# One low half by subtraction on VectorE, and a new order of work on every engine

## The chip, the cores and the metric

The kernel runs on one core of a Trainium2 chip. The metric is the device time of one execution in microseconds, the median of three runs. A profile is one more execution, taken with the hardware profiler; its span runs from the first to the last instruction. Engines: TensorE (PE), VectorE (DVE), ScalarE (ACT), GpSimd (POOL), SyncE (SP, which here only issues transfers).

## The reference

Input `x` is 4 batches of 512 rows by 512, `ctx` 4 batches of 512 by 256. All is float32.

```python
# cross attention
query = ctx @ Wq.T + bq; key = ctx @ Wk.T + bk           # per batch 512 x 128
attention = softmax(query @ key.T)                        # 512 x 512
x = x + layernorm(x) @ attention.T
# feed-forward on 2048 rows, each matrix first rounded block-wise to FP8
def mx_dequant(t):                                        # blocks of 32 along a row
    s = max(max_abs(block) / 448, 1e-30); return fp8_e4m3(t / s) * s
n = layernorm(x)
h = silu(mx(n) @ mx(gate_w).T) * (mx(n) @ mx(up_w).T)     # 2048 x 2048
x = x + mx(h) @ mx(down_w).T
```

## The kernel before

**Units, rows, hidden rows.** The three weight matrices come as twelve `units` of 128 x 2048 (0 to 7 gate and up, in four column groups of 512, two units each; 8 to 11 down). A unit is loaded into one of three buffers `W`, reduced to block maxima (`unit_reduce`, `unit_largest`), scaled (`unit_scale`), rounded to FP8's grid (`unit_round`, after ScalarE's `unit_magnitude`), scaled back (`unit_dequant`). A dequantized value does not fit float16, so it is split: ScalarE writes the high half, minus the value as float16 (`unit_hi`); then value plus high half is left over, and that is the low half. The sum is made by a transfer that GpSimd issues with `accum_op=add` (`unit_rest`), and ScalarE writes it as float16 (`unit_lo`). Both halves are turned by transposing transfers from SyncE (`turn_unit_hi`, `turn_unit_lo`) into `gu_hi`, `gu_lo` or `dn`. The four batches of normalized rows go the same way (`center`, `rows_scale`, `rows_round`, `rows_dequant`, `rows_hi`, `rows_rest`, `rows_lo`, `turn_rows_hi`, `turn_rows_lo`, into `xT`, which has places for two batches), and so do the sixteen hidden row tiles (`hidden_...`, into `hT`, places for two tiles). For hidden tiles 7 to 15 (`hidden_by_vector`) VectorE makes the low half from value and high half by one subtraction, and there is no accumulating transfer. Buffers are shared between the stages, so many waits are on a place that must come free.

**TensorE.** `project`, `energies`, `turn_probs` (transposes the softmax's rows and weighs them) and `attend` are float32 matmuls: attention. `product(r, c)` is row tile r (batch r // 4) times column group c, gate and up, 24 float16 matmuls; it waits for the batch's turned high half, and after 8 matmuls for the low half. `down(r)` is 48 matmuls with hidden tile r. The stages are interleaved: `product(3,0)` is the first product, `product(6,0)` the first with rows of batch 1. Eleven matmuls on zeros stand at the start. All results pass through the eight banks of PSUM; which bank each use takes, and so what it waits for, is written out in `bank_uses`.

**Order.** Each engine has one queue, written out call by call; SyncE's holds all loads, stores and transposes, with waits among them (`sp.wait_ge(*unit_rest_in(4))` ahead of `turn_rows_hi(1)`). GpSimd's holds the maxima over partitions (`unit_max`), the accumulating transfers, `second_norm(b)` (a power, the reciprocal root of batch b's variance, for b from 1), and the accumulating stores of the result (`add_out`). ScalarE makes statistics of x (`row_means`, `row_variances`), the exponentials, `take_probs` (bank to `AT`), `silu_of`. VectorE makes `row_max`, `row_sum`, `add_attended` (x plus attention), `hidden_of` (silu times up). Every wait is a semaphore against a constant count.

The low half's two ways are already there for rows:

```python
def rows_lo_done(b):
    if b in rows_by_vector:
        return nlo_made, ...
    return nlo_ready, ...
```

Of the kernel before, what the change touches and what calls it, by code (L numbers as in the profile page):

```python
# [13 lines left out]
P = 128  # L14
# [18 lines left out]
def xattn_ffn(nc, xrows, xcols, ctxT, consts, units, out):  # L33
# [35 lines left out]
        ("p0.0 p2.0 e2.0 a0.3 a1.0 a2.2 g1.0 a3.2 g2.1 g4.1 u6.2 g0.2 u0.3 u3.3 u7.1 g8.0 u9.1 g11.0 u12.0 u14.2"  # L69
         " u13.1 g8.2 u10.2 u15.0 d9").split(),  # L70
        ("p0.1 e1.0 e2.1 t1.0 a1.1 t3.0 g0.0 u2.0 g4.0 u2.2 g0.1 u6.3 u1.3 g7.1 d0 g9.1 u10.0 d4 g10.3 u15.1 d11").split(),
        ("e0.0 e1.1 t0.3 a0.2 e3.0 t2.2 a2.0 g3.0 u1.0 g6.0 u4.1 u3.2 u0.2 u1.1 g4.3 u7.2 u8.0 g9.3 g11.1 g12.1"
         " g14.2 u13.0 g12.3 u10.1 d6 g15.3 d14").split(),
        ("e0.1 e1.2 a0.0 t1.3 a1.3 t3.3 a3.3 u2.1 g5.0 g5.1 g5.3 g1.2 u4.2 g7.3 g8.1 g9.2 u11.0 u12.1 g14.3 g13.1"
         " u12.3 g10.2 g15.0 u15.2 d13").split(),
        ("e0.2 e1.3 a0.1 t2.0 t2.3 a2.1 u3.0 g2.0 g6.1 u5.0 g5.2 u5.3 g1.3 u4.3 u7.3 g9.0 u9.3 u11.2 u14.1 g13.0"
         " u13.3 g10.1 u11.3 g15.2 d12").split(),
        ("e0.3 t0.0 t0.2 e2.2 t1.1 t2.1 e3.3 t3.1 u0.0 u6.0 g2.2 u5.1 g6.3 u1.2 g7.0 g2.3 u8.1 g10.0 g11.2 u14.0"
         " u12.2 g13.3 u8.3 g11.3 d8 d15").split(),
        ("p1.0 p2.1 t0.1 p3.1 t1.2 a1.2 t3.2 a3.0 g3.1 u6.1 g6.2 u5.2 g0.3 g3.3 u7.0 u2.3 u9.0 d2 d3 g12.0 g14.1"  # L80
         " g12.2 u13.2 g8.3 d5 g15.1 u15.3").split(),
        ("p1.1 p3.0 e2.3 e3.1 e3.2 a2.3 a3.1 u3.1 u4.0 g3.2 u0.1 g1.1 g4.2 g7.2 d1 u9.2 u11.1 g14.0 u14.3 g13.2"
         " u8.2 u10.3 d7 d10").split(),
# [3 lines left out]
    rows_by_vector = ()  # L87
    logged = (0,)
    stats_by_vector = ()
    slice_size = 256  # L90
    hidden_by_vector = (7, 8, 9, 10, 11, 12, 13, 14, 15)

    with ExitStack() as stack:
# [237 lines left out]
        def _(sp):  # L331
# [13 lines left out]

            def load_consts():
                sp.dma_start(late[:, 1024:1538 + P], consts).then_inc(consts_in, 16)
# [114 lines left out]
            turn_unit_hi(0)  # L462
            load_unit(3)
            turn_unit_lo(0)
            load_rows(3)
            store_rows(0)
            sp.wait_ge(*unit_rest_in(1))
            turn_unit_hi(1)
            load_columns(2)
            load_unit(4)  # L470
            turn_unit_lo(1)
            turn_unit_hi(2)
            load_columns(3)
            sp.wait_ge(*rows_rest_in(0))
# [5 lines left out]
            store_rows(2)  # L480
# [3 lines left out]
            load_unit(6)  # L484
            store_rows(3)
# [26 lines left out]
            turn_unit_hi(10)  # L512
            reload_rows(2)
            turn_unit_lo(10)
            turn_unit_hi(11)
            sp.wait_ge(*hidden_rest_in(0))
            turn_unit_lo(11)
# [10 lines left out]
            turn_hidden_hi(2)  # L528
            sp.wait_ge(*hidden_rest_in(3))
            turn_hidden_lo(2)  # L530
            turn_hidden_hi(3)
            turn_hidden_lo(3)
            load_last()
            sp.wait_ge(*rows_rest_in(3))
            turn_hidden_hi(4)
            turn_hidden_lo(4)
            turn_hidden_hi(5)
            turn_rows_hi(3)
            turn_rows_lo(3)
# [11 lines left out]
            turn_hidden_lo(10)  # L551
            turn_hidden_hi(11)
            turn_hidden_lo(11)
# [16 lines left out]
        def _(pool):  # L570
# [34 lines left out]
            unit_max(0)  # L605
            unit_rest(0)
            unit_max(1)
            unit_max(2)
            pool.wait_ge(wT_in[1], 16)
            unit_rest(1)  # L610
            pool.wait_ge(wT_in[0], 48)
            unit_rest(2)
            rows_rest(0)
# [9 lines left out]
            unit_max(6)  # L623
            pool.wait_ge(wT_in[1], 80)
            unit_rest(5)
            unit_max(7)
            pool.wait_ge(wT_in[1], 96)
            unit_rest(6)
            unit_max(8)
            pool.wait_ge(wT_in[1], 112)  # L630
            unit_rest(7)
            unit_max(9)
            pool.wait_ge(wT_in[1], 128)
            unit_rest(8)
# [42 lines left out]
        def _(pe):  # L677
# [104 lines left out]
            energies(0, 0)  # L782
            energies(0, 1)
            energies(0, 2)
            energies(0, 3)
            project(1, 0)
            project(1, 1)
            project(2, 0)
            energies(1, 0)
            project(2, 1)  # L790
            energies(1, 1)
            project(3, 0)
            energies(1, 2)
            energies(1, 3)
            turn_probs(0, 0)
            energies(2, 0)
            turn_probs(0, 1)
            energies(2, 1)
            turn_probs(0, 2)
            turn_probs(0, 3)  # L800
# [3 lines left out]
            attend(0, 1)  # L804
            attend(0, 2)
            energies(2, 3)
            attend(0, 3)
            turn_probs(1, 0)
            turn_probs(1, 1)
# [3 lines left out]
            energies(3, 0)  # L813
            energies(3, 1)
            attend(1, 0)
            attend(1, 1)
            turn_probs(2, 1)
# [4 lines left out]
            energies(3, 2)  # L822
            energies(3, 3)
# [15 lines left out]
            product(2, 0)  # L839
# [38 lines left out]
            product(11, 0)  # L878
            product(11, 1)
            product(11, 2)  # L880
            down(3)
# [20 lines left out]
            down(6)  # L902
            product(15, 0)
            product(15, 1)
            down(7)
            down(8)
            product(15, 2)
# [10 lines left out]
        def _(act):  # L918
# [223 lines left out]
            act.wait_ge(consts_in, 16)  # L1142
            take_projection(0, 0)
            take_projection(0, 1)
            row_means(0, 0)
            row_means(0, 1)
            unit_magnitude(0)
            unit_rescale(0)
            take_projection(1, 0)
            exponential(0, 0)  # L1150
            take_projection(1, 1)
            exponential(0, 1)
            row_variances(0, 0)
# [24 lines left out]
            exponential(2, 0)
            unit_rescale(1)
            exponential(2, 1)  # L1180
            row_variances(0, 1)
            exponential(2, 2)
            row_means(2, 0)
            take_projection(3, 1)
            unit_hi(1)
            weigh(1, 2)
            unit_magnitude(2)
            exponential(2, 3)
            take_probs(1, 0)
            weigh(1, 3)  # L1190
            unit_rescale(2)
            weigh(2, 0)
            take_probs(1, 1)
            take_probs(1, 2)
            take_probs(1, 3)
            weigh(2, 1)
            row_means(3, 0)
            unit_lo(1)
            attended_variances(0, 0)
            row_variances(1, 0)  # L1200
            row_means(2, 1)
            row_variances(2, 0)
            rows_magnitude(0)
            unit_hi(2)
            weigh(2, 2)
            attended_variances(0, 1)
            exponential(3, 0)
            weigh(2, 3)
            take_probs(2, 0)
            exponential(3, 1)  # L1210
            take_probs(2, 1)
            take_probs(2, 2)
            take_probs(2, 3)
            row_variances(1, 1)
            rows_hi(0)
            exponential(3, 2)
            row_means(3, 1)
            row_variances(3, 0)
            exponential(3, 3)
            row_variances(2, 1)  # L1220
            weigh(3, 0)
            weigh(3, 1)
            weigh(3, 2)
            weigh(3, 3)
            unit_magnitude(3)
            rows_lo(0)
# [742 lines left out]
```

## Time and profile before

| | |
|---|---|
| median of three runs | 611.02 us (610.16 to 611.29) |
| the profiled execution | 610.0 us |
| its span | 608.0 us |
| TensorE busy / mean granted clock | 600.6 us (99%) / 0.999 |
| VectorE busy | 484.0 us (80%) |
| ScalarE busy | 309.2 us (51%) |
| GpSimd busy | 44.8 us (7%) |
| matmuls in the trace | 2683 |
| transfers: SyncE's share of 16 engines, GpSimd's | 45.2%, 19.9% |

Busy time of an engine is from its first to last cycle of each instruction; matmuls overlap, and a busy TensorE is one with no hole. VectorE's 80% is an average: it is over 97% in most slices before 260 us and near nothing from 410 to 450.

### The profile page before, as it was taken

The numbers are of one execution on the slowest core, as the hardware profiler recorded it, in microseconds if no ns is written. First come the engines' busy times: TensorE is split into PE (matmuls) and PEld (weight loads), VectorE is DVE, ScalarE is ACT, GpSimd is POOL, SyncE is SP. The second block draws the span as 40 slices with busy tenths as digits, with TensorE's granted clock in tenths as the row PEclk, the third lists the DMA queues.
The fourth block names the chain that finished last, engine by engine and source line by source line (L and its number), as shares of the span: only waits on it lengthen the run. The fifth ranks groups of instructions, "written<-read, shape, count | busy, mean of one in ns | idle before, by whom it ended". The sixth has DMA issues, their size and how long they took to land.

```text
span 608.0 us, 7215 instructions
## 1 busy us (share of the span) xinstructions
PE 600.6 (99%) x2683; PEld 282.3 (46%) x2683; DVE 484.0 (80%) x455; ACT 309.2 (51%) x463; POOL 44.8 (7%) x60
## 2 busy tenths in 40 slices
PE   8999999999999999999999999999999999999998
PEld 3456554444444444444444444444444444444446
DVE  4999998899999999988999985131148899989740
ACT  3999989553555555853475532431121515254520
POOL 0000002100000001010110201000000000001100
PEclk9999999999999999999999999999999999999999
DMA  8989869989988978867445655750010334557691
GB/s 314 396 206 275 234 177 256 280 193 249 208 207 209 219 159 210 174 140 171 124 112 97 148 112 113 165 86 0 1 19 0 53 69 83 90 105 101 110 171 35
DMA packets 148162, 92.28 MB, mean 152 GB/s; under 512 B 134304, under 2 KB 134688, under 8 KB 143264
## 3 DMA queue, kind: packets, MB, share of 16 engines
q1 hardware_dynamic: 142656, 63.78, 45.2%
q0 software_dynamic: 5472, 28.05, 19.9%
q8 instruction: 21, 0.34, 0.2%
q14 instruction: 13, 0.11, 0.1%
HBM read 25.76 MB, written 8.39 MB: 56 GB/s over the span
## 4 chain that ended last, share of the span: by engine, by line
PE 85%; DMA 5%; issue 3%; ACT 3%; DVE 1%; SPq 1%; POOL 0%; DVEq 0%; ACTq 0%
PE bank L727 49%; PE bank L739 17%; PE bank L742 9%; PE bank L711 5%; DMA h<-in_ctxT 2%; PE bank L702 1%; PE bank L695 1%; DMA xT<-hT 1%; PE bank L687 1%; PE bank L757 1%; DMA W<-hT 1%; DMA h<-hT 1%; ACT hT L944 1%; PE bank L762 1%; ACT h L987 0%
## 5 line engine op out<-in xcount | busy, mean ns | idle before, releaser
L727 PE MATMUL bank<-gu_hi,xT 128*128 128x512 f16 x1024 | 243.6, 380 | 1.7 <-DMA xT<-hT 1.7
L727 PEld LDWEIGHTS bank<-gu_hi,xT 128*128 128x128 f16 x1024 | 99.9, 98 | 123.4 <-DMA xT<-hT 3.2
L727 PE MATMUL bank<-gu_lo,xT 128*128 128x512 f16 x512 | 131.5, 379 | 0.0
L739 PE MATMUL bank<-dn,hT 128*128 128x512 f16 x480 | 106.1, 379 | 0.0
L1633 DVE SCALAR_TENSOR_TENSOR h<-bank,unscale,silu 128x512 f32<-128x512 f32 x64 | 47.4, 747 | 56.1 <-PE bank L727 36.1
L1088 ACT ACTIVATE silu<-bank,unscale 128x512 f32<-128x512 f32 x64 | 42.8, 679 | 83.4 <-PE bank L727 40.3
L727 PEld LDWEIGHTS bank<-gu_lo,xT 128*128 128x128 f16 x512 | 50.1, 98 | 60.4
L739 PEld LDWEIGHTS bank<-dn,hT 128*128 128x128 f16 x480 | 47.0, 98 | 56.6
L1114 ACT ACTIVATE W<-h 128x2048 f16<-128x2048 f32 x16 | 30.5, 1909 | 68.3 <-DVE W L1665 25.4
L711 PE MATMUL bank<-dn,h 128*128 128x512 f32 x128 | 55.9, 593 | 0.0
L742 PE MATMUL bank<-dn,hT 128*128 128x512 f16 x240 | 54.3, 379 | 0.0
L1458 DVE SCALAR_TENSOR_TENSOR h<-mag,h 128x2048 f32<-128x2048 bf16 x18 | 41.2, 2288 | 9.4 <-ACT mag L926 9.4
L926 ACT ACTIVATE mag<-h 128x2048 bf16<-128x2048 f32 x18 | 34.2, 1903 | 19.5 <-DVE h L1647 14.1
L1459 DVE SCALAR_TENSOR_TENSOR h<-mag,h 128x2048 f32<-128x2048 bf16 x18 | 41.2, 2292 | 0.6
L926 ACT ACTIVATE mag<-W 128x2048 bf16<-128x2048 f32 x14 | 26.7, 1908 | 23.0 <-DVE W L1590 11.9
L711 PEld LDWEIGHTS bank<-dn,h 128*128 128x128 f32 x128 | 24.3, 190 | 29.8 <-issue 29.4
L1665 DVE SCALAR_TENSOR_TENSOR W<-h,W 128x2048 f16<-128x2048 f32 x9 | 20.6, 2289 | 20.9 <-DMA hT<-W 17.4
L1647 DVE TENSOR_TENSOR h<-h,rscale 128x2048 f32<-128x2048 f32 x16 | 36.7, 2292 | 0.5
L1642 DVE TENSOR_REDUCE hscale<-h 128x64 f32<-128x2048 f32 x16 | 36.5, 2281 | 0.3
L1659 DVE TENSOR_TENSOR h<-h,hscale 128x2048 f32<-128x2048 f32 x16 | 36.6, 2288 | 0.2
L742 PEld LDWEIGHTS bank<-dn,hT 128*128 128x128 f16 x240 | 23.5, 98 | 28.3
L1458 DVE SCALAR_TENSOR_TENSOR W<-mag,W 128x2048 f32<-128x2048 bf16 x14 | 32.0, 2286 | 1.0 <-ACT mag L926 1.0
(119 smaller groups left out, 560.1 us busy)
## 6 DMA issues: line engine op xcount, KB each, us to landing
W<-hT POOLq DMA_DIRECT2D x12, 1024.0 KB, 5.9
W<-in_units SPq DMA_DIRECT2D x11, 1024.0 KB, 5.7
h<-W POOLq DMA_DIRECT2D x7, 1024.0 KB, 6.1
h<-in_xcols SPq DMA_DIRECT2D x4, 1024.0 KB, 12.6
out_y<-y POOLq DMA_DIRECT2D x12, 256.0 KB, 6.2
h<-in_xrows SPq DMA_DIRECT2D x2, 1024.0 KB, 11.8
out_y<-h SPq DMA_DIRECT2D x2, 1024.0 KB, 5.5
h<-hT POOLq DMA_DIRECT2D x2, 1024.0 KB, 5.9
```

The source lines that it names most:

```text
L711: last = pe.matmul(bank[:, :], xTf[b % 2][:, j, lt * P:(lt + 1) * P], AT[:, j, :], start=(j == 0), stop=(j == HT - 1))
L727: last = pe.matmul(bank[:, :], xT[:, b % 2, part, k, :], w[:, c, g, j * 512:(j + 1) * 512], start=(j == 0 and not low), stop=(j == HT - 1 ...
L739: pe.matmul(bank[:, :], hT[:, r % 2, 0, k, :], dn[:, w, k, :], start=(k == 0 and w == 0), stop=False)
L742: last = pe.matmul(bank[:, :], hT[:, r % 2, 1, k, :], dn[:, 0, k, :], start=False, stop=(k == IT - 1))
L926: nc.scalar.activation(mag[:, :], v, ACT.Abs, scale=MAGIC).then_inc(mag_ready, 1)
L1088: nc.scalar.activation(silu[:, n % 2, :], bank_of(f"g{r}.{c}")[:, :], ACT.Silu, scale=unscale[:, 2 * c:2 * c + 1]).then_inc(silu_ready, 1)
L1458: then(dve.scalar_tensor_tensor(v, mag[:, :], floor, v, ALU.max, ALU.add))
L1459: dve.scalar_tensor_tensor(v, mag[:, :], floor, v, ALU.max, ALU.subtract).then_inc(mag_used, 1)
L1633: dve.scalar_tensor_tensor(hrow(r)[:, c * 512:(c + 1) * 512], bank_of(f"u{r}.{c}")[:, :], unscale[:, 2 * c + 1:2 * c + 2], silu[:, n % 2, ...
L1642: then(dve.tensor_reduce(s, blocks(row), AX.X, ALU.max, apply_absolute_value=True))
L1647: dve.tensor_tensor(blocks(row), blocks(row), each_block(rscale[:, :]), ALU.mult).then_inc(hv_ready, 1)
L1659: dve.tensor_tensor(blocks(row), blocks(row), each_block(hscale[:, r % 2, :]), ALU.mult).then_inc(hd_ready, 1)
```

## The change

Batch 0's rows join `rows_by_vector`: VectorE runs its `rows_lo(0)` (shown below), GpSimd's `rows_rest(0)` and ScalarE's `rows_lo(0)` are gone, and SyncE no longer waits for `rows_rest_in(0)`. A switch `apart`, left off, could load part of the constants first. And the calls on all five queues, with the banks, are in a new order; no call but those named is added or removed. At the start, the constants are loaded ahead of the first context tile, and the other context tiles ahead of the rows:

```diff
-    rows_by_vector = ()
+    rows_by_vector = (0,)
@@ SyncE
 load_slice(0)
+load_consts()
 load_ctx(0)
-load_consts()
 load_half(0)
 load_rest(0)
-load_rows(0)
 load_ctx(1)
 load_unit(1)
+load_ctx(2)
 load_ctx(3)
-load_ctx(2)
+load_rows(0)
+load_columns(0)
 load_rows(1)
+load_rows(2)
 load_unit(2)
-load_columns(0)
-load_rows(2)
 load_columns(1)
...
+sp.wait_ge(*unit_rest_in(2))
 turn_unit_hi(2)
-load_columns(3)
-sp.wait_ge(*rows_rest_in(0))
 turn_rows_hi(0)
 turn_rows_lo(0)
 store_rows(1)
 turn_unit_lo(2)
 load_unit(5)
-store_rows(2)
 sp.wait_ge(*unit_rest_in(3))
 turn_unit_hi(3)
 turn_unit_lo(3)
 load_unit(6)
+store_rows(2)
 store_rows(3)
 sp.wait_ge(*unit_rest_in(4))
 turn_rows_hi(1)
@@ GpSimd
-pool.wait_ge(wT_in[0], 48)
+pool.wait_ge(wT_in[1], 32)
 unit_rest(2)
-rows_rest(0)
@@ TensorE
+turn_probs(3, 0)
+turn_probs(3, 1)
 attend(2, 0)
 ...
 attend(2, 3)
-turn_probs(3, 0)
-turn_probs(3, 1)
 turn_probs(3, 2)
-turn_probs(3, 3)
 product(3, 0)
 product(1, 0)
+turn_probs(3, 3)
 product(0, 0)
+product(2, 0)
 attend(3, 0)
 ...
 attend(3, 3)
-product(2, 0)
@@ VectorE
 rows_round(0)
+unit_power(3)
 rows_dequant(0)
 add_attended(1, 0)
 ...
 add_attended(1, 3)
+rows_lo(0)
+attended_means(1)
 unit_reduce(4)
...
 rows_dequant(1)
+unit_power(4)
+add_attended(2, 1)
 unit_round(4)
-hidden_of(3, 0)
+add_attended(2, 2)
+add_attended(2, 3)
 unit_dequant(4)
...
 hidden_of(15, 3)
+hidden_scale(15)
 hidden_round(14)
+hidden_lo(13)
 hidden_dequant(14)
-hidden_scale(15)
-hidden_lo(13)
 hidden_round(15)
```

The subtraction that VectorE now runs for batch 0, in code that was there and unused:

```python
def rows_lo(b):
    dve.wait_ge(nhi_ready, b + 1)
    if b % 2 == 1:
        dve.wait_ge(nT_in[1], 16 * b)
    parts = xparts_of(b)
    dve.scalar_tensor_tensor(parts[:, 1, :], xw_of(b), -1.0, parts[:, 0, :],
                             ALU.mult, ALU.subtract).then_inc(nlo_made, 1)
```

Between `silu_of(3,0)` and batch 1's variance ScalarE's new order is: `silu_of(3,0)`, `center_by_scalar(1,1)`, `take_probs(3,1)`, `take_probs(3,2)`, `weigh(3,3)`, `unit_hi(3)`, `attended_variances(1,0)`, `attended_variances(1,1)`. Before, it was `silu_of(3,0)`, `take_probs(3,0)`, `attended_variances(1,0)`, `unit_hi(3)`, `take_probs(3,1)`, `attended_variances(1,1)`, with both halves of `center_by_scalar(1)` ahead.

## Rows read from the trace of the kernel before

**Rows 1.** page, part 1: TensorE's busy time
```profile
PE 600.6 (99%) x2683; PEld 282.3 (46%) x2683; DVE 484.0 (80%) x455; ACT 309.2 (51%) x463; POOL 44.8 (7%) x60
```

**Rows 2.** TensorE in order of time: start, length, line, count, [idle before, releaser]
```profile
18.58 1.96 PE L687 MATMUL bank<-h,gu_lo 128*128 128x512 f32 x4 [0.79 <-DMA h<-in_ctxT]
...
35.24 10.46 PE L711 MATMUL bank<-dn,h 128*128 128x512 f32 x24
...
74.20 13.90 PE L711 MATMUL bank<-dn,h 128*128 128x512 f32 x32
87.94 3.73 PE L702 MATMUL bank<-h,gu_lo 128*128 128x128 f32 x32
92.60 1.04 PE L727 MATMUL bank<-gu_hi,xT 128*128 128x512 f16 x4 [0.93 <-DMA xT<-hT]
...
94.99 1.90 PE L727 MATMUL bank<-gu_hi,xT 128*128 128x512 f16 x8 [0.49 <-DMA xT<-hT]
...
138.57 1.04 PE L727 MATMUL bank<-gu_hi,xT 128*128 128x512 f16 x4 [0.32 <-DMA xT<-hT]
```

**Rows 3.** the chain that ended last: start, length, what
```profile
77.34 5.10 issue
82.44 5.75 DMA h<-hT
...
104.51 6.03 issue
...
124.79 5.83 DMA W<-hT
130.63 7.89 DMA xT<-hT
138.57 134.85 PE bank L727 x624
...
584.23 6.91 PE bank L739 x32
```

**Rows 4.** ScalarE in order of time, around batch 1's variance
```profile
75.44 1.89 ACT L1074 ACTIVATE hT<-h 128x2048 f16<-128x2048 f32 x1
...
92.34 2.54 ACT L1059 ACTIVATE h<-h,nmean 128x512 f32<-128x512 f32 x4
...
96.70 1.28 ACT L1088 ACT_TABLE_LOAD   x1
...
104.29 0.21 ACT L1044 ACTIVATE var<-ysum 128x4 f32<-128x4 f32 x1
```

**Rows 5.** GpSimd in order of time: start, length, line, [idle before]
```profile
71.57 0.85 POOL L585 DMA_DIRECT2D W<-hT  x1 [23.09 <-DMA gu_hi<-hT]
82.44 0.88 POOL L589 DMA_DIRECT2D h<-hT  x1 [10.01 <-issue]
...
110.53 1.89 POOL L580 TENSOR_TENSOR rstd<-var,mhalf 128x4 f32<-128x4 f32 x1 [6.75 <-issue]
```

**Rows 6.** the twelve accumulating transfers of `unit_rest` (L585), issue to landing
```profile
DMA to landing us min/median/max: 5.8/5.9/10.6
```

**Rows 7.** page, part 5: groups, busy us, mean ns of one
```profile
L926 ACT ACTIVATE mag<-W 128x2048 bf16<-128x2048 f32 x14 | 26.7, 1908 | 23.0 <-DVE W L1590 11.9
...
L1665 DVE SCALAR_TENSOR_TENSOR W<-h,W 128x2048 f16<-128x2048 f32 x9 | 20.6, 2289 | 20.9 <-DMA hT<-W 17.4
```

**Rows 8.** VectorE in order of time, its two longest holes before 123
```profile
106.88 2.29 DVE L1458 SCALAR_TENSOR_TENSOR h<-mag,h 128x2048 f32<-128x2048 bf16 x1 [2.31 <-ACT mag L926]
...
112.52 0.23 DVE L1549 TENSOR_TENSOR xscale<-xscale,rstd 128x64 f32<-128x64 f32 x1 [1.02 <-POOL rstd L580]
```

**Rows 9.** SyncE's queue at the end: hidden row 14, high and low
```profile
577.65 3.19 SPq L439 DMA_TRANSPOSE hT<-W  x1
580.93 1.93 SPq L444 DMA_TRANSPOSE hT<-W  x1
```

**Rows 10.** the four transposes of rows' high halves (L420), issue to landing
```profile
DMA to landing us min/median/max: 4.3/4.6/7.9
```

More of the change, by code:

```diff
@@ L804, in _ @@
             attend(0, 1)
+            energies(2, 3)
+            turn_probs(1, 0)
+            energies(3, 0)
             attend(0, 2)
-            energies(2, 3)
+            turn_probs(1, 1)
+            energies(3, 1)
             attend(0, 3)
-            turn_probs(1, 0)
-            turn_probs(1, 1)
             turn_probs(1, 2)
@@ L812, in _ @@
             turn_probs(2, 0)
-            energies(3, 0)
-            energies(3, 1)
+            turn_probs(2, 1)
+            energies(3, 2)
             attend(1, 0)
+            energies(3, 3)
             attend(1, 1)
-            turn_probs(2, 1)
             attend(1, 2)
@@ L901, in _ @@
             product(11, 3)
-            down(6)
             product(15, 0)
             product(15, 1)
+            down(6)
+            product(15, 2)
             down(7)
             down(8)
-            product(15, 2)
             down(9)
@@ L1197, in _ @@
-            row_means(3, 0)
+            exponential(3, 0)
+            row_means(2, 1)
+            unit_rescale(2)
+            exponential(3, 1)
+            weigh(2, 2)
+            attended_variances(0, 0)
+            weigh(2, 3)
+            row_variances(1, 1)
             unit_lo(1)
-            attended_variances(0, 0)
-            row_variances(1, 0)
-            row_means(2, 1)
+            exponential(3, 2)
             row_variances(2, 0)
+            exponential(3, 3)
+            unit_hi(2)
@@ L1231, in _ @@
-            unit_lo(2)
-            silu_of(3, 0)
-            take_probs(3, 0)
+            unit_magnitude(3)
+            row_variances(3, 1)
+            take_probs(3, 0)
+            unit_lo(2)
+            center_by_scalar(1, 0)
+            silu_of(3, 0)
+            center_by_scalar(1, 1)
+            take_probs(3, 1)
+            take_probs(3, 2)
+            weigh(3, 3)
+            unit_hi(3)
             attended_variances(1, 0)
-            unit_hi(3)
-            take_probs(3, 1)
             attended_variances(1, 1)
-            take_probs(3, 2)
+            silu_of(1, 0)
@@ L1366, in _ @@
-            hidden_rescale(7)
-            hidden_hi(6)
-            silu_of(11, 2)
+            hidden_lo(4)
+            take_down(2)
+            hidden_magnitude(6)
+            hidden_rescale(5)
+            hidden_rescale(6)
+            hidden_hi(5)
+            rows_lo(3)
+            silu_of(11, 0)
+            hidden_lo(5)
+            hidden_unscale(3)
+            silu_of(11, 1)
+            hidden_unscale(4)
+            hidden_magnitude(7)
+            hidden_rescale(7)
+            hidden_unscale(5)
@@ L1439, in _ @@
             take_down(14)
+            hidden_unscale(15)
         @block.vector
@@ L1684, in _ @@
             unit_scale(0)
-            unit_power(0)
+            unit_reduce(1)
             row_max(0, 0)
@@ L1758, in _ @@
             add_attended(3, 2)
+            hidden_of(1, 0)
             add_attended(3, 3)
-            hidden_of(1, 0)
+            unit_reduce(6)
+            hidden_of(0, 0)
             unit_scale(5)
-            hidden_of(0, 0)
-            unit_reduce(6)
+            unit_largest(6)
+            unit_scale(6)
+            unit_power(5)
             unit_round(5)
-            unit_largest(6)
-            unit_power(5)
-            unit_scale(6)
             unit_dequant(5)
@@ L1771, in _ @@
             unit_round(6)
+            hidden_of(2, 1)
             unit_reduce(7)
-            hidden_of(2, 1)
+            hidden_of(6, 0)
+            hidden_of(6, 1)
             unit_largest(7)
@@ L1777, in _ @@
             unit_dequant(6)
-            hidden_of(6, 0)
+            unit_power(7)
             unit_round(7)
-            hidden_of(6, 1)
             unit_reduce(8)
```

520 lines of the change are left out of this document (249 added, 271 removed).

## The prediction

> **What bounds the kernel now.** I read the page's busy times first, then who waited for whom, then TensorE's order of time, and last the chain followed back from the end. TensorE is busy 600.6 of 608.0 us and its mean granted clock is 0.999 (the 2.4 GHz level) [rows 1]. No edit adds or removes a matmul, so the time after is TensorE's work plus its holes. The holes that an order can fill are few: 0.79 us for the third context tile (`ctx(2)`), 0.93 and 0.49 at the first `product(3,0)` (both for batch 0's transposed rows), and 0.32 at 138.57, where `product(6,0)` waits for batch 1's transposed rows [rows 2]. After 138.57 there is none. So the end is fixed by when `product(6,0)` starts, provided that nothing later is late; I call that time T. It is 138.57 before. The profiled execution took 610.0 us with a span of 608.0, and the three timed runs have a median of 611.02: I add a change of T to the median. 0.2% of that is 1.2 us, about what a measurement can tell from no change.
>
> The chain says what T hangs on [rows 3]: batch 1's variance leaves ScalarE at 104.5; GpSimd's power starts 6.03 us later and takes 1.90; then (from 112.5) VectorE dequantizes the rows, rounds and dequantizes unit 4; ScalarE writes unit 4's high half; the accumulating transfer takes 5.83; and only behind that transfer does SyncE issue `turn_rows_hi(1)`, whose transpose lands after 7.89. Once T has come, TensorE runs on at 134.85 us for 26 products, 5.18 each. This is a chain of VectorE and transfers under a TensorE that looks full.
>
> **The change, part by part.** (1) Batch 0's low half. Removed: `rows_rest(0)`, issued at 82.44 although ScalarE's high half was written at 77.3 [rows 4]. It stood 5.10 us behind GpSimd's previous transfer, `unit_rest(2)`, issued at 71.57 and landing 10.6 us later, at 82.2; then it took 5.75 itself [rows 3, 5, 6]. Removed too: ScalarE's `rows_lo(0)`, 1.90 us. Added: a subtraction on VectorE, 2.29 us, the price of the nine of that form [rows 7]. So the low half is ready one pass (2.2 us, back to back) behind the high half instead of 10.85 + 1.9. The Trainium skill (DMA: Bandwidth & Descriptors, Issuing engines are not separate DMA queues) says that transfers from all engines run on the same 16 DMA engines and interleave. By that rule `rows_rest(0)` should have started at 77.3 and shared; the trace disagrees for these two, since the second starts only when the first has landed. By the rule the removal saves the transfer alone (5.75), by the row 10.85; neither alters T, which is batch 1's.
>
> (2) VectorE has 5.88 us of holes between 10 and 122.4 (0.98, 0.76, 0.57, 0.24, 2.31, 1.02; the largest in [rows 8]), and is otherwise full there, so the added 2.2 us must fit in these holes or delay everything behind it.
>
> (3) The orders on five queues. Contexts 1 to 3 are loaded ahead of the rows, which removes the 0.79: `project(2,0)` now comes after energies(1,1), at about 19.3, and its tile ends 3.98 MB into SyncE's queue instead of 5.56 (sums of the tiles' sizes). I walked the new order by hand, with durations from before: projection 1.72 and energies 0.86 (four and two matmuls of 0.43, the spacing of attend's 32 in 13.74), attend 3.44, turn_probs 0.92, product 5.18; 2.2 per big VectorE pass and 1.8 per ScalarE pass (the mean less 0.1, since passes overlap at their ends), 0.6 from the end of matmuls to their reader [rows 2, 3, 7]. `attend(0,0)` comes out at about 34.3 (35.24 before), and `product(3,0)` at S = 92.60 - 0.93 - 0.79 - 0.92 (turn_probs(3,3) is moved behind two products) = 90.0. Batch 0's rows: VectorE now does unit 3's scale, row maxima and rows_scale(0) in another order, `rows_dequant(0)` ends at 79.9 (73.1 before), the high half at 82.6, the subtraction at 84.9. SyncE first waits for `unit_rest(2)` (80 to 82), turns unit 2, and then turns the rows: hi lands at about 88.5, lo at 91. They are wanted at 90.0 and 91.7. So the 0.93 and 0.49 go too, with about a microsecond to spare. TensorE's lead when it comes to `product(6,0)` is 0.79 + 0.93 + 0.49 + 0.32 = 2.5, so it could start it at 136.0.
>
> (4) But batch 1's chain. Before, ScalarE's queue took 104.50 - 96.70 = 7.8 from the table load of silu(3,0) to the variance [rows 4]. The new order has the same work in it and half a centering more (2.54 / 2, 1.22 net) and one weigh (0.29): 9.3. It begins when the gate is there, S + 2.6 + 0.6 = 93.2, so the variance leaves at 102.5, 2.0 before its old time. GpSimd: +6.03 + 1.90 = 110.4. VectorE is free by then (rows_round(1) ends at 109.8). It then does rows_dequant(1) 2.47, unit_power(4) 0.27, add_attended(2,1) 0.75, unit_round(4) 4.53, two add_attended 1.34, unit_dequant(4) 2.20 = 11.56: 122.0. Before, the same stretch held only hidden_of(3,0) between them, so 1.7 of the 2.0 gained is given back by the three additions and the power. unit_hi(4) 1.92 and 0.37 to the issue: 124.3; +5.83 = 130.1; +7.89 = T = 138.0 [rows 3, 5]. I add 0.6 for the couplings of the walk that were within 0.4 us (attend(1,0), turn_probs(3,0) and attend(2,0) each wait on a ScalarE instruction that ends 0.2 to 0.4 before it is wanted), and 0.2 for `store_rows(2)`, which now leaves at 120 and not at 104.6, 7.3 us long alone, mostly over before unit 4's transfer moves data. T = 138.8.
>
> New waits on the way: attend(3,2) needs the bank that add_attended(2,2) frees at 119.4, and TensorE comes there at 118.5; 0.9 us, but it comes out of the lead of 2.5 and costs nothing. load_unit(3) now waits for unit_lo(0), which is at 43.8 instead of 38.8, while unit_reduce(3) moves from 73.1 to 50.2: 43.9 + 5.7 = 49.6, so 0 if it lands so, 1 to 2 us of VectorE if not.
>
> (5) Everything behind 140 moves little. Walked in the same way: VectorE ends unit 5's dequantization at 144.1 in both; rows 2 are turned about 4 us later, but their transpose (280.5 and 282.4 before) still lands about 289 and 292, wanted at 294.0 and 295.7; batch 3's comes earlier. The end is the closest: hidden row 14 is turned high at 577.65 and wanted at 584.07, low at 580.93 and wanted at 590.97, with 4.5 to land [rows 3, 9]. In the new order hidden_scale(15) precedes round(14), but rows 8 to 13 run ahead, and I get the high half out at 575.9 and lo at 583.1, so 3 us to spare each. Cost zero; if VectorE were 4 us later, it would be 1 us.
>
> **The rivals.** *The lead is given back* (my forecast): T = 138.8, so +0.2: 611.2. It holds for T between 137.4 and 139.7. *The lead is kept*: the transpose of batch 1 lands in 4.6 us, the median of its four, and not 7.9 [rows 3, 10]. Then T = 138.8 - 3.3 = 135.5, TensorE is the later at 136.0 and the time is 611.0 - 2.5 = 608.5; half of it (T = 137.4) decides for faster. Against it: store_rows(3) still leaves at 127, just ahead of it. *The chain is later*: an accumulating transfer takes 10.6 as `unit_rest(2)` did and not 5.8 [rows 6]. On unit 4 that puts T at 138.8 + 4.8 = 143.6 and the time at 616.0; on unit 2 it is what I counted. A part of it, 0.9 us or more (unit 3's load late, batch 0's transposes late, so that S and all behind it move), decides for slower: T = 139.7 to 141.5, 612.2 to 613.9. *The change does nothing* for the stalls at product(3,0): unit_rest(2) lands after 84 and SyncE holds the rows behind it; then S = 91.4, the chain moves with it, T = 139.5 to 140.2, 612.0 to 612.6.
>
> The Trainium skill (GPSIMD Engine Reference, Specifications) says that GpSimd's SBUF interfaces contend with VectorE instructions that have two SBUF inputs. The added subtraction is one more, so at most its own 2.3 us on a transfer then being set up; here GpSimd has none pending at 82.7, and no term hangs on it.
>
> **How the numbers follow.** Lead given back 0.40, kept 0.28, later 0.22, nothing gained at product(3,0) 0.10. The walk is some 300 steps, each good to 0.1 us, so both sides are open. Faster by over 1.2 us: 0.28, from the second. Within: 0.40 from the first, and 0.03 of the last. Slower: the rest, 0.29. The likeliest time is 611.2, its own range 609.8 to 612.2. The range is 608.7 to 614.8: down to the full lead (608.5) less a hair, up to most of a slow transfer (616.0) cut, which leaves out 2 in 10.
>
> **What would show it.** Right: the wait for ctxT (0.79) gone; attend(0,0) at 34 to 34.6; product(3,0) near 90 with little wait; power of batch 1 at 108 to 109; unit 4's accumulating transfer at 124 to 125; one wait for xT at `product(6,0)`, now 1.5 to 3 us, the new first stall of size; no wait after it. Wrong: a wait of ScalarE or VectorE before attend(2,0), a wait of TensorE after 140, above all at dn/hT near 553 to 595, or unit 4's transfer before 123.

## The result, and the profile after

Before 609.88 us (21 runs, 608.36 to 611.29), after 611.74 us (21 runs, 610.37 to 613.63); ratio 1.0034, 95% interval 1.0025 to 1.0043. The kernel became 0.34% slower, some 2 us, where no measurable change was forecast (611.2 on a median of 611.02). One of e3's twelve runs below (631.0 us, clock 0.949) and one of e8's (910.7 us, clock 0.656) fell into a slower state of the chip and stay out of every median, ratio and count. The profiled execution of after took 613.63 us with a span of 611.8 (before 610.0 and 608.0).

The head first: the page's busy times, then TensorE in order of time up to `product(6,0)`.

```profile
PE 602.4 (98%) x2683; PEld 282.5 (46%) x2683; DVE 486.8 (80%) x456; ACT 306.7 (50%) x462; POOL 53.3 (9%) x59
```

```profile
34.50 7.03 PE L721 MATMUL bank<-dn,h 128*128 128x512 f32 x16
...
89.81 1.03 PE L737 MATMUL bank<-gu_hi,xT 128*128 128x512 f16 x4
...
118.96 7.13 PE L721 MATMUL bank<-dn,h 128*128 128x512 f32 x16 [0.50 <-DVE dn L1513]
...
137.20 1.04 PE L737 MATMUL bank<-gu_hi,xT 128*128 128x512 f16 x4 [0.75 <-DMA xT<-hT]
```

TensorE is busy 1.8 us longer than in [rows 1] with the same 2683 matmuls; the clock, below, accounts for 1.7 of it. The first `attend` stands at 34.50 (before 35.24), `product(3,0)` (L737) at 89.81 with no wait (before 92.60 with 0.93), and T, the start of `product(6,0)`, is 137.20 (before 138.57, [rows 2]). So 1.4 us were won by T. The chain into T, start, length, what:

```profile
121.81 1.92 ACT hT L954
123.73 0.29 issue
124.02 6.14 DMA W<-hT
130.17 0.02 issue
130.18 6.97 DMA xT<-hT
```

The same two transfers as in [rows 3] lead to T, 6.14 and 6.97 long.

The 0.50 at 118.96 is the wait for a bank that the prediction put at 0.9; it comes out of the lead.

Now who TensorE waited for in the whole span: instruction, releaser, us in total, times, longest.

```profile
PE bank L749 <- DMA hT<-W: 2.6, 1, 2.6
PE bank L786 <- DVE dn L1689: 1.2, 1, 1.2
PE bank L705 <- ACT gu_lo L966: 0.8, 1, 0.8
PE bank L737 <- DMA xT<-hT: 0.7, 1, 0.7
```

The largest is new: before had no wait behind T. It is in `down` (L749 the high half's 32 matmuls, L752 the low half's 16), near the end, TensorE in order of time:

```profile
572.37 7.07 PE L749 MATMUL bank<-dn,hT 128*128 128x512 f16 x32
579.92 3.63 PE L752 MATMUL bank<-dn,hT 128*128 128x512 f16 x16 [0.48 <-DMA hT<-W]
586.13 8.75 PE L749 MATMUL bank<-dn,hT 128*128 128x512 f16 x32 [2.59 <-DMA hT<-W]
594.72 3.62 PE L752 MATMUL bank<-dn,hT 128*128 128x512 f16 x16
```

Read it so: `down(13)` starts 1.3 us ahead of before's, waits 0.48 for its low half; `down(14)` waits 2.59 for its high half; and its 32 matmuls then take 8.75 where the 32 above took 7.07. The last group of matmuls begins at 606.91 (before 603.16): -1.37 + 0.48 + 2.59 + 1.68 = +3.4 of the +3.75. In what follows `hi(r)` and `lo(r)` are the two halves of hidden tile r: on ScalarE and VectorE the step that makes one, on SyncE the transpose that turns it; `scale(r)`, `round(r)`, `dequant(r)` and `magnitude(r)` are short for the tile's `hidden_...` steps. SyncE's queue shows why TensorE waits (L444 turns a high half, L449 a low half); the rows are `lo(13)`, `hi(14)` and `lo(14)`.

```profile
575.58 1.32 SPq L449 DMA_TRANSPOSE hT<-W  x1
579.73 3.04 SPq L444 DMA_TRANSPOSE hT<-W  x1
586.84 3.06 SPq L449 DMA_TRANSPOSE hT<-W  x1
```

`hi(14)` goes out at 579.73 (before 577.65 [rows 9], walked 575.9). VectorE's holes from 485 to 545, in order of time, are where it lost the time:

```profile
488.68 2.29 DVE L1467 SCALAR_TENSOR_TENSOR h<-mag,h 128x2048 f32<-128x2048 bf16 x1 [2.10 <-ACT mag L936]
...
534.65 2.29 DVE L1674 SCALAR_TENSOR_TENSOR W<-h,W 128x2048 f16<-128x2048 f32 x1 [3.69 <-ACT W L1124]
542.25 2.29 DVE L1674 SCALAR_TENSOR_TENSOR W<-h,W 128x2048 f16<-128x2048 f32 x1 [5.30 <-DMA hT<-W]
```

L1674 is the subtraction for a hidden tile: `lo(10)` waits for ScalarE's high half, and `lo(11)`, right behind it in the new order, waits through ScalarE for the transpose of `hi(10)`. That makes three suspects: the new order of the ends of the queues as a whole, one of its pieces (transposes, `lo(11)`, `hidden_scale(15)` ahead of `round(14)`), or the new head.

In the matmuls after the wait the granted clock shows. The columns of the row are the window, its length, busy us and count of each engine, PEclk, DMA share and GB/s.

```profile
580.00:586.00 6.00, 3.55 (x16) 1.39 (x16) 5.97 (x3) 2.73 (x8) 1.76 (x2) 1.00 1.07 163
586.00:592.00 6.00, 5.87 (x20) 2.39 (x21) 0.86 (x2) 3.30 (x5) 0.86 (x1) 0.72 1.04 162
592.00:598.00 6.00, 6.00 (x30) 2.68 (x29) 2.25 (x1) 0.00 (x0) 0.00 (x0) 1.00 1.12 175
```

PEclk is 1.00 (the 2.4 GHz level), 0.72 in the window behind the hole, a mixture with the 1.2 GHz level, and 1.00 again. Of after's 21 runs, six have a mean clock of 0.997 and a median of 613.3 us; the other fifteen, at 0.999 or 1.0, have a median of 611.4.

### The profile page after: what moved, and what is told of

The parts are those of the page before. It is cut to its first block, busy times and chain, and to the rows that moved or that the text cites. A ratio compares the mean times of both kernels' runs of the same rounds, so it can differ in the third digit from the quotient of the medians.

```text
span 611.8 us, 7218 instructions
## 1 busy us (share of the span) xinstructions
PE 602.4 (98%) x2683; PEld 282.5 (46%) x2683; DVE 486.8 (80%) x456; ACT 306.7 (50%) x462; POOL 53.3 (9%) x59
## 4 chain that ended last, share of the span: by engine, by line
PE 77%; DVE 10%; DMA 5%; issue 4%; ACT 2%; SPq 1%; DVEq 0%; ACTq 0%
PE bank L737 48%; PE bank L749 8%; PE bank L721 8%; PE bank L752 4%; PE bank L697 2%; PE bank L712 2%; PE bank L705 2%; DVE h L1656 2%; DVE h L1467 2%; DVE hscale L1651 2%; DMA hT<-W 2%; PE bank L767 1%; DVE h L1468 1%; DMA xT<-hT 1%; DVE W L1674 1%
## 5 line engine op out<-in xcount | busy, mean ns | idle before, releaser
L737 PE MATMUL bank<-gu_hi,xT 128*128 128x512 f16 x1024 | 243.7, 379 | 0.7 <-DMA xT<-hT 0.7
L737 PEld LDWEIGHTS bank<-gu_hi,xT 128*128 128x128 f16 x1024 | 100.0, 98 | 121.9 <-DMA xT<-hT 1.6
L737 PE MATMUL bank<-gu_lo,xT 128*128 128x512 f16 x512 | 131.4, 379 | 0.0
L749 PE MATMUL bank<-dn,hT 128*128 128x512 f16 x480 | 107.7, 383 | 2.6 <-DMA hT<-W 2.6
L737 PEld LDWEIGHTS bank<-gu_lo,xT 128*128 128x128 f16 x512 | 50.1, 98 | 60.4
L749 PEld LDWEIGHTS bank<-dn,hT 128*128 128x128 f16 x480 | 47.3, 99 | 60.7 <-issue 5.4
L752 PE MATMUL bank<-dn,hT 128*128 128x512 f16 x240 | 54.3, 379 | 0.5 <-DMA hT<-W 0.5
L1674 DVE SCALAR_TENSOR_TENSOR W<-h,W 128x2048 f16<-128x2048 f32 x9 | 20.6, 2289 | 24.6 <-DMA hT<-W 20.9
L752 PEld LDWEIGHTS bank<-dn,hT 128*128 128x128 f16 x240 | 23.4, 98 | 29.1 <-DMA hT<-W 1.0
```

Source lines behind the costliest of these rows:

```text
L737: last = pe.matmul(bank[:, :], xT[:, b % 2, part, k, :], w[:, c, g, j * 512:(j + 1) * 512], start=(j == 0 and not low), stop=(j == HT - 1 ...
L749: pe.matmul(bank[:, :], hT[:, r % 2, 0, k, :], dn[:, w, k, :], start=(k == 0 and w == 0), stop=False)
L752: last = pe.matmul(bank[:, :], hT[:, r % 2, 1, k, :], dn[:, 0, k, :], start=False, stop=(k == IT - 1))
```

## The experiments

"The ends" are the calls on SyncE, TensorE, ScalarE and VectorE from `down(5)` (about 465 us) on, with the banks of those products and downs. Ratios are to the kernel before.

### e1_tail_before: the change with the old ends

```diff
@@ all four queues from down(5) on, and bank_uses for them
-(order of the changed kernel)
+(order of the kernel before)
```

> The changed kernel with the end of all five queues (from down(5) on) in the old order. Theory A (the new order of the end costs what the head gained): no hole in TensorE after 140, product(6,0) at 137.2 as in the changed kernel, down(14) at 582.7, and the time 1.4 us below before, ratio 0.9977. Theory B (the end is late whatever its order, because TensorE now comes 1.4 us earlier and every transfer behind it does not): a hole of 1 us or more at down(14) stays, ratio 1.000 or above.

Measured: 608.22 us (607.77 to 608.93, 12 runs), ratio 0.9978 (0.9968 to 0.9989). The start of `product(6,0)` is 136.44, and the end has no hole; TensorE in order of time:

```profile
571.57 7.07 PE L742 MATMUL bank<-dn,hT 128*128 128x512 f16 x32
578.48 3.62 PE L745 MATMUL bank<-dn,hT 128*128 128x512 f16 x16
581.93 7.07 PE L742 MATMUL bank<-dn,hT 128*128 128x512 f16 x32
```

So subtraction and new head together gain 0.22%, and the new ends cost 1.0034 / 0.9978 = 0.56%, 3.4 us. What follows takes each side apart.

### e2_scale15_later: one piece, hidden_scale(15)

```diff
@@ VectorE
-hidden_scale(15)
 hidden_round(14)
 hidden_lo(13)
 hidden_dequant(14)
+hidden_scale(15)
@@ ScalarE
-hidden_magnitude(15)
 take_down(10)
 hidden_unscale(14)
 hidden_hi(14)
+hidden_magnitude(15)
```

> The changed kernel; only hidden_scale(15) moved back behind round(14), lo(13) and dequant(14) on VectorE, and ScalarE's magnitude(15) behind hi(14). Theory A with this one step as the cause: dequant(14) ends 5.7 us earlier (at 572.0), its high half is turned at about 574.5, the hole of 2.6 at down(14) is gone; down(15) might wait up to 1 us for its own half; ratio 0.998 to 1.000. Rival (the end is late since hidden rows 8 to 12, upstream of it): the hole moves to down(15) and keeps 2 us or more, ratio 1.002.

Measured: 615.07 us (614.37 to 616.28, 6 runs), ratio 1.009 (1.007 to 1.011): worse, a miss. `hi(14)` went out at 575.14, 4.6 us earlier, and the hole at it is gone; but `scale(15)` had now joined `round(15)` and `dequant(15)` between `dequant(14)` and `lo(14)`, and that half, issued at 589.91 (586.84 in the changed kernel), was waited for instead:

```profile
582.61 7.07 PE L749 MATMUL bank<-dn,hT 128*128 128x512 f16 x32
594.46 5.27 PE L752 MATMUL bank<-dn,hT 128*128 128x512 f16 x16 [4.77 <-DMA hT<-W]
```

The 16 matmuls behind the hole took 5.27 us against 3.62. So VectorE's lateness at 575 is older than this piece: shifting work between two steps of it only chooses who waits.

### e3_hi_first: two pairs of transposes in the old order

```diff
@@ SyncE
-turn_hidden_lo(7)
 turn_hidden_hi(7)
+turn_hidden_lo(7)
...
-turn_hidden_lo(11)
 turn_hidden_hi(11)
+turn_hidden_lo(11)
```

> The changed kernel; only SyncE's order: hidden tile 7's high half turned before its low half, and the same for tile 11. If the two waits of VectorE that my walk missed or undersized (2.1 us at 488.7 behind ScalarE's high half of tile 8, and 5.3 at 542) come from this, VectorE is 2 to 4 us earlier at dequant(14), the hole at down(14) shrinks from 2.6 to under 1, ratio 0.998 to 1.001. If not, ratio 1.0034 as the changed kernel.

Measured: 610.33 us (median of 11 runs), ratio 1.0008 (0.9994 to 1.0021). `hi(14)` goes out at 577.58, and the hole shrinks to 1.66 with the clock kept:

```profile
583.97 7.07 PE L749 MATMUL bank<-dn,hT 128*128 128x512 f16 x32 [1.66 <-DMA hT<-W]
```

### e10_hi7_alone: only the first of the two pairs

```diff
@@ SyncE
-turn_hidden_lo(7)
 turn_hidden_hi(7)
+turn_hidden_lo(7)
```

> The changed kernel with hi(7) before lo(7) on SyncE, and lo(11) still before hi(11). Theory A (the 2.10 us of VectorE at 488.7 come of hi(7) being transposed behind lo(7), and are the larger part of what e3 regained): that hole falls under 0.5 us, hi(14) issued at 577.5 to 578.2 instead of 579.7, the hole at down(14) 1.0 to 1.8 us, the clock not lower, 610.2 to 610.8 us, ratio 1.0003 to 1.0018. Rival (it is hi(11) that mattered): the hole at down(14) stays above 2.2 us and the ratio at 1.003 or more.

Measured: 610.20 us (609.75 to 611.56, 12 runs), ratio 1.0017 (1.0004 to 1.003). The hole of 2.10 us on VectorE is gone, `hi(14)` goes out at 577.98, and the hole at `down(14)` is 1.65. So `hi(7)` accounts for all that e3 regained, and `hi(11)` for nothing: counted from T, `hi(14)` goes out after 440.9 us in both. How much was regained is less sure. It is 1.6 us against after's profiled run (442.5 us from T), but 0.9 against that of e4_fill (441.8), which has after's orders up to there. ScalarE's high half of tile 8 needs the buffer that `turn_hidden_hi(7)` reads, and one transpose put ahead of it passed its 2 us through ScalarE to VectorE; 0.9 to 1.6 of them reached the end, 90 us later.

### e9_lo11_later: e3, and lo(11) away from lo(10)

```diff
@@ VectorE
 hidden_lo(10)
-hidden_lo(11)
 hidden_of(15, 2)
 hidden_dequant(12)
 hidden_round(13)
+hidden_lo(11)
 hidden_dequant(13)
```

> e3_hi_first with one more move: VectorE's lo(11) no longer right behind lo(10) but behind of(15, 2), dequant(12) and round(13). In e3 VectorE stood 5.95 us at 540.1 for ScalarE's hi(11), which itself waited for the transpose of hi(10). Theory A (VectorE lost its lead in that standstill; the work moved in front fills it): its later steps 4 to 6 us earlier, hi(14) issued at 572 to 574 instead of 577.6, no hole at down(14), 608.2 to 609.0 us, ratio 0.9975 to 0.999. Rival (VectorE's backlog is set elsewhere, by ScalarE's late magnitudes and scale(15) ahead of round(14)): hi(14) at 576 or later, the hole stays over 0.8 us, 609.8 to 610.8 us, ratio 0.9995 to 1.0015.

Measured: 608.00 us (607.84 to 609.12, 12 runs), ratio 0.9974 (0.9965 to 0.9984), the lowest median measured here and faster than both kernels (its interval overlaps those of e1_tail_before and e5_subtraction_alone). VectorE in order of time, the subtractions for tiles 10, 11 and 12:

```profile
532.18 2.29 DVE L1674 SCALAR_TENSOR_TENSOR W<-h,W 128x2048 f16<-128x2048 f32 x1 [3.69 <-ACT W L1124]
...
541.78 2.28 DVE L1674 SCALAR_TENSOR_TENSOR W<-h,W 128x2048 f16<-128x2048 f32 x1
543.98 2.28 DVE L1668 TENSOR_TENSOR h<-h,hscale 128x2048 f32<-128x2048 f32 x1
548.45 2.29 DVE L1674 SCALAR_TENSOR_TENSOR W<-h,W 128x2048 f16<-128x2048 f32 x1 [2.19 <-DMA hT<-W]
```

The hole of 5.95 us at `lo(11)` in e3 is filled with the work moved ahead of it; 2.19 come back at `lo(12)`. Net 3.6 (3.9 counted from T): `hi(14)` goes out at 574.01 instead of 577.58, and TensorE has no wait behind T. The 3.69 at `lo(10)` is still there, and so is `hidden_scale(15)` ahead of `round(14)`: with the lead back, both cost nothing.

### e8_vector_end: e3, and the end of VectorE's order by a second rule

```diff
@@ VectorE, behind hidden_of(15, 3)
-scale(15) round(14) lo(13) dequant(14) round(15) dequant(15) lo(14) lo(15)
+round(14) dequant(14) lo(13) scale(15) lo(14) round(15) dequant(15) lo(15)
@@ ScalarE
 (magnitude(15) behind hi(14), as in e2_scale15_later)
```

> e3_hi_first plus another end of VectorE's order: round(14), dequant(14), lo(13), scale(15), lo(14), round(15), dequant(15), lo(15), with ScalarE's magnitude(15) behind hi(14). Theory A (the remaining 1.66 us hole is scale(15) ahead of round(14), and e2_scale15_later missed because round(15) and dequant(15) then stood ahead of lo(14)): hi(14) is issued about 5 us earlier than in e3 (577.6), lo(14) at about 578 to 580 instead of 584.7, no wait of TensorE above 0.5 us behind 540, 608.2 to 608.9 us, ratio 0.9975 to 0.999. Rival (VectorE is short of time whatever the order): the hole moves to down(15) or its low half, ratio 1.000 or more.

Measured: 609.65 us (median of 11 runs), ratio 1.0004 (0.9992 to 1.0016). The theory missed: `hi(14)` gained only 0.4 us (577.18), `lo(14)` 1.6, and the waiting moved to tile 15 (L767). That is seen in the profiled execution, whose 612.86 us are the longest of the eleven:

```profile
PE bank L767 <- DMA hT<-W: 2.9, 1, 2.9
PE bank L772 <- DMA hT<-W: 0.8, 1, 0.8
```

The waits fell where the rival put them, but its reason, that VectorE is short of time, does not hold either. VectorE stood 5.32 us ahead of `round(14)` for ScalarE's `magnitude(14)`, and ScalarE was late because its `hi(13)`, shortly ahead in its queue, had waited 10.71 us for a transpose (VectorE's row first, then ScalarE's):

```profile
565.98 2.29 DVE L1467 SCALAR_TENSOR_TENSOR h<-mag,h 128x2048 f32<-128x2048 bf16 x1 [5.32 <-ACT mag L936]
```

```profile
561.74 1.91 ACT L1124 ACTIVATE W<-h 128x2048 f16<-128x2048 f32 x1 [10.71 <-DMA hT<-W]
```

So the place of `scale(15)` was filled by a hole of about its length. Beside e9, this says that the end of VectorE's order was not the fault; the lead lost before 545 was.

### e7_before_with_new_ends: the kernel before with the new ends

```diff
@@ all four queues from down(5) on, and bank_uses for them
-(order of the kernel before)
+(order of the changed kernel)
```

> The kernel before with the new order of the five queues' ends from down(5) on, and nothing else. Theory A (the ends alone cost the time): TensorE waits for hi(14) here too, about 1.4 us less than in the changed kernel since TensorE itself comes 1.4 us later: a hole of 1 to 2.2 us at down(14), ratio 1.002 to 1.005. Rival (the new ends are only bad behind the new head, by what they find in the queues): no hole above 0.5 us, ratio 0.999 to 1.001.

Measured: 612.97 us (612.36 to 615.27, 6 runs), ratio 1.0056 (1.0044 to 1.0068). The ends alone cost it, as expected, but more than I wrote (the profiled execution took 615.27 us, the longest of the six):

```profile
580.82 3.63 PE L735 MATMUL bank<-dn,hT 128*128 128x512 f16 x16 [0.43 <-DMA hT<-W]
587.49 8.75 PE L732 MATMUL bank<-dn,hT 128*128 128x512 f16 x32 [3.04 <-DMA hT<-W]
```

I had reckoned with a hole 1.4 us smaller, since TensorE comes later. `product(6,0)` starts at 138.19, 1.0 later than in the changed kernel, and `hi(14)` goes out at 580.65, 0.9 later: the whole tail, VectorE's part too, rides on TensorE's pace. I take the reason to be that its last tiles are made from the last products; no run tests that alone. e6 below shows the same with the old ends: T comes 6.44 us later than in e1, and `hi(14)` 6.44 later (581.96 for 575.52). A gain at the head hardly widens or narrows a hole at the end (3.04 here, 2.59 in after).

### e5_subtraction_alone: the subtraction in the old orders

```diff
-rows_by_vector = ()
+rows_by_vector = (0,)
@@ VectorE
 add_attended(1, 3)
+rows_lo(0)
@@ GpSimd
-rows_rest(0)
@@ ScalarE
-rows_lo(0)
@@ SyncE
-sp.wait_ge(*rows_rest_in(0))
+sp.wait_ge(*unit_rest_in(2))
```

> The kernel before with the subtraction alone: VectorE makes batch 0's low half behind add_attended(1, 3), the accumulating transfer and ScalarE's step go, SyncE waits for unit 2's transfer instead, and every order stays. The first transpose of batch 0's rows then needs only unit 2's transfer (71.6 + 10.6 us), not the one queued behind it (82.4 + 5.8), so TensorE's waits of 0.93 and 0.49 us at the first products go, and ScalarE is no longer held until 88.2. Theory A (the subtraction pays by itself): the first product at 91.6 instead of 92.6, product(6, 0) 0.8 to 1.7 us earlier than 138.57, and the whole lead kept, since the old order of the ends is the one that kept it: ratio 0.997 to 0.999. Rival (the walked orders are what gains the head): VectorE's 2.3 us more eat the lead in batch 1's chain, product(6, 0) at 138.3 to 139.0, ratio 0.9995 to 1.001.

Measured: 608.55 us (607.80 to 608.99, 11 runs), ratio 0.9982 (0.9974 to 0.9991). TensorE in order of time at the first product and at T:

```profile
91.88 1.03 PE L726 MATMUL bank<-gu_hi,xT 128*128 128x512 f16 x4
...
137.07 1.04 PE L726 MATMUL bank<-gu_hi,xT 128*128 128x512 f16 x4 [0.21 <-DMA xT<-hT]
```

Both waits at the first products are gone, T is 137.07, and VectorE's added 2.3 us went into its holes. The subtraction by itself gives 1.3 us. What the new head adds is not clear of the noise: 0.3 us by the medians (1.6 us in e1), with overlapping intervals.

### e6_orders_alone: the new head with the accumulating transfer

Based on e1_tail_before; batch 0's low half is again the transfer's and ScalarE's.

```diff
-rows_by_vector = (0,)
+rows_by_vector = ()
@@ GpSimd
 unit_max(3)
+rows_rest(0)
@@ ScalarE
 unit_lo(2)
+rows_lo(0)
@@ SyncE
+sp.wait_ge(*rows_rest_in(0))
 turn_rows_hi(0)
@@ VectorE
-rows_lo(0)
```

> The version of e1_tail_before without the subtraction: the new orders of the head, the old ends, and batch 0's low half again by the accumulating transfer on GpSimd (behind unit_max(3)), ScalarE's step behind unit_lo(2) and SyncE's wait for the transfer. rows_hi(0) ends at 82.0 in the new order and such a transfer took 5.75 us, so the transpose starts at about 88.2 instead of 82.1 and lands at about 92.7, where product(3, 0) stood at 89.8. Theory A (the new order needs the subtraction): product(3, 0) 2.5 to 3.5 us later, product(6, 0) at 138.5 to 140, ratio 1.000 to 1.003. Rival (the orders alone gain the head): product(6, 0) below 138, ratio 0.9975 to 0.999.

Measured: 614.25 us (613.87 to 614.62, 5 runs), ratio 1.0077 (1.0065 to 1.0089), worse than either theory. TensorE in order of time:

```profile
91.75 1.04 PE L732 MATMUL bank<-gu_hi,xT 128*128 128x512 f16 x4 [2.56 <-DMA xT<-hT]
92.63 1.46 PE L732 MATMUL bank<-gu_lo,xT 128*128 128x512 f16 x4
96.87 3.38 PE L732 MATMUL bank<-gu_hi,xT 128*128 128x512 f16 x8 [2.79 <-DMA xT<-hT]
...
142.88 1.04 PE L732 MATMUL bank<-gu_hi,xT 128*128 128x512 f16 x4 [0.38 <-DMA xT<-hT]
```

`product(3,0)` comes at 91.75, 2.7 us later than in e1 (89.04), as expected; what I left out is the low half, 2.79 us more, and 1.5 us of lower clock behind them (8 matmuls in 3.38 against 1.90). T is 142.88, 6.4 us behind e1's. The new head is no gain of its own: it is an order made for the subtraction, and with the transfer in it, put where it fits these queues, it costs 6 us.

### e4_fill: matmuls in the standstill

Ten matmuls on data at hand, into `down(14)`'s bank, which its own first matmuls overwrite, ahead of its wait.

```diff
 bank = take_bank(f"d{r}")
+if r == RT - 2:
+    for _ in range(10):
+        pe.matmul(bank[:, :], dn[:, 0, 0, 0:P], dn[:, 0, 0, :], start=True, stop=True)
 pe.wait_ge(hT_in[0], 16 * (r + 1))
```

> The changed kernel with ten extra float16 128x512 matmuls (2.2 us) on down(14)'s own bank ahead of its wait, whose result is overwritten. If the lower granted clock behind the hole (8.75 us for 32 matmuls instead of 7.07 in the profiled run) comes from TensorE standing still, it is gone: 32 matmuls take 7.07 again, the mean clock is 1.000 in all runs, no run above 612.5, and the median is 0 to 1 us below the changed kernel. If the hole is what it is and the clock falls for another reason, the matmuls stay at 8.75 and runs near 613.4 stay.

Measured: 611.37 us (610.24 to 612.64, 12 runs), ratio 1.0027 (1.0014 to 1.0041); no run below a clock of 0.999. One run is above the 612.5 that I had set as the most.

```profile
582.12 2.32 PE L745 MATMUL bank<-dn 128*128 128x512 f16 x10
584.74 7.08 PE L752 MATMUL bank<-dn,hT 128*128 128x512 f16 x32 [0.30 <-DMA hT<-W]
```

The fill takes 2.32 of the standstill, and the 32 matmuls take 7.08. The median is that of after's fifteen runs whose clock did not fall (611.4). So the fall in clock (1.7 us, six runs of 21) goes with the standstill, and the standstill itself is most of the loss. Alone, 0 of 12 runs against 6 of 21 is a difference that chance gives about once in twenty; e1, e5 and e9, which have no standstill, add 0 of 35.

## Why the number came near and the reason did not hold

**Steps (1) and (2) held.** The subtraction fits VectorE's holes, and without the queued transfer the first products wait for nothing. The text said that neither price "alters T, which is batch 1's". That was wrong: in e5 the subtraction alone brings T from 138.57 to 137.07. ScalarE no longer stands behind the low half's step, and unit 3's high half reaches its accumulating transfer at 101.0 instead of 102.9. That is 0.9 of the 1.5 us (unit 4's transfer starts at 123.89 for 124.79); the rest is the transpose behind it, 7.3 for 7.9. I had not walked the old order with the subtraction in it.

**Steps (3) and (4) held to 1.6 us.** `attend(0,0)` 34.50 for 34.3, `product(3,0)` 89.81 for 90.0, unit 4's transfer at 124.02 for 124.3 and 6.14 long for 5.83, one wait at T, though 0.75 us long and not 1.5 to 3. T was 137.20 for 138.8: 0.8 us were my margins, 0.92 the transpose (6.97 for 7.89). Of the 2.5 us of lead 1.4 were kept, near the middle between the forecast and the second rival. By the prediction's own bound (137.4) T falls on the second rival's side. One term of the walk was too high with no effect on T: unit 2's transfer, counted as landing at 80 to 82 since it had taken 10.6 [rows 6], let SyncE go on at 77.5. The twelve of its kind now take 5.7 to 7.0:

```profile
DMA to landing us min/median/max: 5.7/6.1/7.0
```

**Step (5) failed**: "Everything behind 140 moves little", "3 us to spare each; if VectorE were 4 us later it would be 1 us". The high half of tile 14 was walked out at 575.9 and went at 579.73, and its transpose took 6.27 us (the chain's row below), not 4.5.

```profile
579.73 6.27 DMA hT<-W
```

The slack for the high half was 584.3 - 575.9 - 4.5 = 3.9 us (584.3 is before's 584.07 with the forecast T). VectorE was 3.8 later, the transpose 1.8 longer and T 1.6 earlier than walked, 7.2 together and so 3.3 more than the slack; TensorE waited 3.1 (0.48 and 2.59). Had the slack been right, the time would have been 609.88 - 1.4 = 608.5 on the measured median of before; e1, with the old ends, measured 608.22. What the runs show in the place of the slack:
- 0.9 to 1.6 us: `lo(7)` turned ahead of `hi(7)` (e10).
- 3.6 us: `lo(11)` right behind `lo(10)`, where VectorE stands for a transpose (e9: 577.58 to 574.01).
- `hidden_scale(15)` ahead of `round(14)`, the only piece of the ends that the text named: no fault of its own (e9 has it and has no hole; e2 and e8 undo it and do not mend it).
- `hi(11)` behind `lo(11)`: nothing (e3 against e10).
- 1.7 us of lower clock behind the hole in six runs of 21, which no step had.

The prediction gives no figure for the two waits of the first two items; it says only that "rows 8 to 13 run ahead". Both are waits of an engine for a buffer that a *transpose* must have read, carried by way of ScalarE. A walk that follows only operations and their inputs passes over them. The last condition was also mis-set: I took the slack against a TensorE that moves by itself, but e7 shows the tail riding along with T.

**The rivals.** None of the four is what happened: in all of them T decides the time. The closest in time is "the change does nothing", which gave 612.0 to 612.6 for stalls that stay at `product(3,0)`, where the stalls in fact went and T was earlier. The test that the prediction named for its being wrong, "a wait of TensorE after 140, above all at dn/hT near 553 to 595", is what the profile shows. The time, 611.74, lies in the range and 0.5 us from the likeliest value, and that is luck: 1.4 us gained at T take back part of the 3.4 lost behind it, neither of them forecast, and before's median, to which the forecast was added, came to 609.88 and not 611.02. The change itself is +1.9 us where +0.2 was forecast, beyond the 1.2 us that were to tell "slower", a side that had 0.29.

## What to carry to other kernels

- When a change gains a little at the head and rewrites the order of everything, put the old tail back behind the new head: one run told the gain (1.6 us) from the loss (3.4 us), and the change proper, alone in the old order, was worth 1.3.
- In a walk, follow each buffer back to the transfer that reads it last. A step that needs such a buffer, placed with nothing between it and the step before, turns the transfer's whole latency into a standstill (4.6 to 6.0 us at `lo(11)` here), and the bill may come 40 to 90 us later on another engine.
- A lead of a few us at the end is spent on whichever piece is late first; undoing the piece next to the hole (e2, e8) moves it to the next half or tile. Look upstream for the engine's own holes.

## What the runs showed of the hardware

The granted clock of TensorE fell behind some standstills and not behind others, most of them near the end. Behind the 2.6 us hole of after in 6 of 21 runs (32 matmuls in 8.75 us for 7.07 in the profiled one, PEclk 0.72); with the 4.8 us hole of e2 in 6 of 6; with e7's of 3.0 in 2 of 6; with two holes of 2.6 and 2.8 within 6 us in e6 in 5 of 5; with the holes of 1.7 in e3 and e10 in 1 of 23; with the hole filled (e4) or absent (e1, e5, e9) in 0 of 47. The profiled run of e8, with its hole of 2.9 at tile 15, kept its clock, as did the other ten. The kernel before, whose profile has no hole there, shows such a clock too, in 2 of the 75 runs whose clock is on record (612.05 and 612.09 us). On the whole longer holes go with more such runs, and each fall costs about 1.7 us on top.

Unit 2's accumulating transfer took 10.6 us before [rows 6]. It was not the transfer queued behind it: with that one gone and the old loads, in e5, the longest of the twelve is still 10.5, and with batch 0's transfer kept and the new head, in e6, it is 6.8. The rows are issue to landing, e5 first, e6 second.

```profile
DMA to landing us min/median/max: 5.8/5.9/10.5
```

```profile
DMA to landing us min/median/max: 5.8/6.0/6.8
```

So the new head made it quick. In both heads the same load of 1 MB (`in_xcols`) runs beside it. Where the transfer was issued 0.74 us behind that load (before, e5, e7) it took 10.3 to 10.6 us; where it was issued about 1.3 us ahead of the load (every other version) it took 6.8 to 7.4. Whether that order is the cause, no run tests by itself.

The Trainium skill says (DMA: Bandwidth & Descriptors, Issuing engines are not separate DMA queues), as weighed in step (1), that transfers from all engines run on the same 16 DMA engines. The traces agree as far as a transfer is slowed by others beside it.

The wait of 5.10 us ahead of `rows_rest(0)` comes again in e7, which has the head of before (4.78 us), and nowhere else. It is not what every accumulating transfer behind a running one does: in the same trace of before, GpSimd issued a hidden tile's accumulating transfer at 296.75 (such a one takes 5.7 us or more to land) and an accumulating store 0.56 us later. What held `rows_rest(0)` stays open.

```profile
296.75 0.86 POOL L593 DMA_DIRECT2D h<-W  x1 [21.14 <-ACT W L1114]
297.31 1.22 POOL L600 DMA_DIRECT2D out_y<-y  x1
```
